# Attention with sixteen channels: the vector engine's pieces start two channels ahead, are computed with integer bit operations, and take 512 more columns

## The chip, the core and the metric

The kernel runs on one core of a Trainium2 chip. The metric is the device time of one execution in microseconds. The core has TensorE (PE, matrix products), VectorE (DVE), ScalarE (ACT, activation functions), GpSimd (POOL) and SyncE (SP, which issues DMAs). They run side by side and wait for each other through semaphores.

## The reference

What matters is the attention layer; a small feed-forward layer with experts follows it.

```python
cos_pm = jnp.cos(phase_modulators)              # 16 channels x 16 heads
def wl_step(acc, wl):
    cpm, iw = wl
    m = cpm[None, :, None, None]
    scores = jnp.einsum('bhqd,bhkd->bhqk', Q * m, K * m) * SCALE
    scores = scores * jnp.cos(KERR * scores * scores)
    attn = jax.nn.softmax(scores, axis=-1)
    out = jnp.einsum('bhqk,bhkd->bhqd', attn, V)
    return (acc + out * iw, None)
acc, _ = jax.lax.scan(wl_step, acc0, (cos_pm, interference_weights))
```

There are 8 batches, 16 heads, 512 positions and 8 dimensions per head. The cosine of the scores is one in single precision for these inputs, and the kernel has a branch for that case, which is the one that runs. So each channel w is exp(scores * c2[w, head]), normalised and multiplied by V: 16 exponentials of the same scores with different scales.

## The kernel before

**Units.** The work is cut into 32 units of one head and four batches: units 0 to 15 for the first four batches, 16 to 31 for the second four. A unit's scores lie in `s_t` as 8192 columns on 128 partitions (4 tiles of 128 keys, times 4 batches, times 512 queries), in one of two buffers. A unit has 15 steps, w = 0 to 14, one for each channel that ScalarE does.

**ScalarE.** At step w it computes the exponential of channel w into one of two buffers of `probs`: all 8192 columns for w = 0 to 13 (line 694). For w = 14 it computes fewer (line 691), `ACT_LAST`: 6144 in units 0 to 15, 6656 in units 16 to 31. Before it writes, it waits until TensorE has used the buffer's previous content, that of channel w - 2 (`pv_done`); before a unit it waits for the unit's scores (`st_copied`).

**VectorE's pieces.** Channel 15, and what ScalarE leaves of channel 14, are computed on VectorE by `piece_dve` in pieces of up to 2048 columns: four for channel 15 and a fifth for channel 14 (2048 or 1536 columns). A piece is seven operations, numbered 0 to 6 (lines 764, 767, 771, 775, 779, 783, 787): split the scaled score in a whole number and a fraction (0 to 2), a polynomial of the fraction (3 to 5), times the power of two (6). The pieces of a unit are numbered through, 35 operations, and a table says which of them stand in which step:

```python
PIECE_STEPS = {0: (0, 3), 1: (3, 5), 2: (5, 6), 3: (6, 8), 4: (8, 10), 5: (10, 12), 6: (12, 15), 7: (15, 18), 8: (18, 19),
               9: (19, 21), 10: (21, 22), 11: (22, 24), 12: (24, 27), 13: (27, 31), 14: (31, 35)}
PRODUCT_STEPS = {6: 0, 8: 1, 11: 2, WA: 3, WA + 1: 4}
COPY_STEPS = {2: 0, 5: 1, 8: 2, 11: 3, WA: 4, WA + 1: 5}
TURN_STEPS = {4: 0, 7: 1, 10: 2, 13: 3, WA + 1: 4, WA + 2: 5}
```

A step of WA (15) or more is one of the next unit.

**TensorE.** At step w it does the pieces' products that are due (`piece_pe`, line 800), then waits for ScalarE's channel w and does its 16 matmuls of 512 columns (line 1392; the trace records each matmul twice, so they are x32 there). Then it transposes a finished group of three channels (`turn_products`, line 1362), which VectorE has copied out of PSUM before (`copy_products`, line 1524) and normalises after (`weigh`, lines 1534 to 1552), and last it does its part of the preparation of the next unit.

**Preparation of the next unit.** It goes back and forth between TensorE and VectorE: projections (lines 829 and 906) at step 1, four score tiles and their maxima (846, 911) at steps 2 to 5, transposes at step 6 (852, 859; 915, 918), and four tiles of final scores and their copies to `s_t` (886, 923) at steps 8 to 11.

**Feed-forward in units 16 to 31.** The layer behind the attention is done for the first batches in between, at fixed steps (`FF_STEPS`). VectorE waits there for a short chain on GpSimd (lines 532 to 544) before line 1006.

Each engine runs its instructions strictly in the order in which the program writes them: in a step of VectorE, pieces, copies, `weigh`, preparation.

Of the kernel before, what the change touches and what calls it, by code (L numbers as in the profile page):

```python
# [15 lines left out]
P = 128  # L16
# [26 lines left out]
SHARED_B = (0, 1)  # L43
ACT_LAST = [T * X_COLS - (NB - b) * S for b in SHARED_B]
PIECES = T + 1
# [63 lines left out]
def postln_kernel(nc, a):  # L109
    with ExitStack() as ctx:  # L110
# [23 lines left out]
        x_2k = sb("x_2k", [P, X_COLS], BF16)  # L134
        x_n = x_2k[:].bitcast(I16)
# [82 lines left out]
        gate_b = scratch(G + EXPERTS)  # L218
        assert taken[0] <= T * NB * S
# [8 lines left out]
        one_row = sb("one_row", [P, P])  # L228
# [279 lines left out]
        def _(pool):  # L508
# [3 lines left out]
            nc.gpsimd.memset(one_row[:], 1.0)  # L512
# [241 lines left out]
        def piece_dve(dve, n, op, u, p, h):  # L754

            piece, base = u * PIECES + n, (u * PIECES + n) * PIECE_LINKS

            w, start, cols = (W - 1, n * X_COLS, X_COLS) if n < T else (WA - 1, ACT_LAST[u // H], T * X_COLS - ACT_LAST[u // H])
            scores = s_t[:, p, start:start + cols]
            scale = c2_last[:, w - (WA - 1), h:h + 1]  # L760
            at, y, t = x_n[:, 0:cols], x_y[:, 0:cols], x_p[:, piece % 2, 0:cols]
# [23 lines left out]
            if op == 6:  # L785
                dve.wait_ge(s["piece_chain"], base + 5)
                nc.vector.scalar_tensor_tensor(out=t, in0=t, scalar=EXP2_D, in1=x_2k[:, 0:cols], op0=ALU.add, op1=ALU.mult) \  # L787
                    .then_inc(s["piece_ready"], 1)

        def piece_pe(pe, n, u):  # L790

            pe.wait_ge(s["piece_ready"], u * PIECES + (n + 2))
# [553 lines left out]
        def _(pe):  # L1346
# [8 lines left out]
            with pe.If(fast == 1):  # L1355
# [10 lines left out]
                for u in range(UNITS):  # L1366
# [12 lines left out]

                    for w in range(WA):  # L1380
# [8 lines left out]
                        for kt in range(T):  # L1389
                            for b in range(SHARED_B[g] if w == WA - 1 and kt == T - 1 else NB):  # L1390
# [5 lines left out]
                                    stop=(w in LAST_OF and kt == (T - 2 if u == UNITS - 1 and w == WA - 1 and b >= SHARED_B[g] else T - 1)))  # L1396
# [24 lines left out]
        def _(dve):  # L1421
# [91 lines left out]
            with dve.If(fast == 1):  # L1513
                def copy_products(v, at):

                    wg = GROUP_AT[at]
                    if wg == NWG - 1:
                        dve.wait_ge(s["piece_used"], v * PIECES + (T + 1))
                    else:

                        dve.wait_ge(s["pv_done"], v * WA + (sum(W_GROUPS[wg]) + 3))
                        if wg == LAST_OF[WA - 1]:
                            dve.wait_ge(s["piece_used"], v * PIECES + (PIECES + 1))
# [35 lines left out]
                for u in range(UNITS):  # L1559
# [68 lines left out]
```

## Time and profile before

| | |
|---|---|
| three runs | 3397.57, 3400.41, 3402.31 us, median 3400.41 |
| the profiled execution | 3401.9 us, its span 3400.1 us |
| busy | ACT 98%, DVE 95%, PE 78%, POOL 7% |
| ScalarE, line 694 | 447 activations of 8192 columns |
| TensorE's mean granted clock | 0.942 of full speed |

The span is the time from the first to the last instruction of the profile. The loop over the units lies between about 38 us and 3320 us; some 80 us of feed-forward layer follow.

### The profile page before, as it was taken

How to read it: one execution, taken by the hardware profiler on the slowest of the kernel's cores; microseconds unless marked ns; L12 is line 12 of the kernel's file. 1: busy time of each engine (PE TensorE's matmuls, PEld its weight loads, DVE VectorE, ACT ScalarE, POOL GpSimd, SP SyncE). 2: the span in 40 equal slices, each digit the busy share in tenths (PEclk: the TensorE clock that was granted, in tenths of full speed). 3: DMA queues.
4: the chain of work that ended last, by engine and by line, in shares of the span. 5: the costliest groups of instructions: out<-in, count | busy, mean ns of one | idle time of the engine just before them, and what ended most of it. 6: DMA issues, size and time to landing. Idle time of an engine off the chain costs nothing.

```text
span 3400.1 us, 47604 instructions
## 1 busy us (share of the span) xinstructions
PE 2635.9 (78%) x20641; PEld 755.2 (22%) x20641; DVE 3235.6 (95%) x2740; ACT 3316.0 (98%) x612; POOL 230.5 (7%) x321
## 2 busy tenths in 40 slices
PE   7777877777777777777777778788888777777776
PEld 2212222212221222221222222222222222222224
DVE  7999999999999999999999999999999999999997
ACT  7999999999999999999999999999999999999992
POOL 0000000000000000000001111101111101111000
PEclk8999899999999989999999999988999999999988
DMA  1000000000000000000000000000000000000001
GB/s 50 1 1 1 1 1 1 1 1 1 1 1 1 1 1 1 1 15 1 1 1 3 4 2 4 2 1 4 2 4 3 4 1 2 4 2 16 1 18 31
DMA packets 21400, 16.05 MB, mean 5 GB/s; under 512 B 4865, under 2 KB 19602, under 8 KB 20946
## 3 DMA queue, kind: packets, MB, share of 16 engines
q1 hardware_dynamic: 19922, 12.28, 1.2%
q8 instruction: 165, 2.70, 0.3%
q10 hardware_dynamic: 1152, 0.53, 0.1%
q0 software_dynamic: 128, 0.26, 0.0%
q14 instruction: 33, 0.27, 0.0%
HBM read 7.70 MB, written 5.37 MB: 4 GB/s over the span
## 4 chain that ended last, share of the span: by engine, by line
ACT 59%; issue 33%; ACTq 4%; DVE 2%; PE 2%; DMA 0%; POOL 0%; DVEq 0%
ACT probs L694 55%; ACTq L684 4%; ACT probs L691 3%; PE psum L1392 0%; ACTq L688 0%; DVE s_t L923 0%; DMA probs<-in_L_attn_bv_dram 0%; DVE m_pad L911 0%; DVE probs L976 0%; DVE probs L1006 0%; PE psum L950 0%; PE psum L945 0%; PE psum L1093 0%; PE psum L935 0%; PE psum L1112 0%
## 5 line engine op out<-in xcount | busy, mean ns | idle before, releaser
L694 ACT ACTIVATE probs<-s_t 128x8192 f32<-128x8192 f32 x447 | 3100.4, 7070 | 2.5 <-PE psum L1392 2.5
L1392 PE MATMUL psum<-probs,v_pad 128*27 128x512 f32 x15136 | 1889.3, 640 | 644.2 <-ACT probs L694 609.2
L1392 PEld LDWEIGHTS psum<-probs,v_pad 128*27 128x27 f32 x15136 | 458.4, 112 | 1990.1 <-issue 1007.6
L767 DVE SCALAR_TENSOR_TENSOR x_y<-s_t,c_last,x_2k 128x2048 f32<-128x2048 f32 (+1 forms) x160 | 369.5, 2310 | 2.4
L779 DVE SCALAR_TENSOR_TENSOR x_p<-x_p,x_y 128x2048 f32<-128x2048 f32 (+1 forms) x160 | 358.2, 2239 | 4.5
L787 DVE SCALAR_TENSOR_TENSOR x_p<-x_p,x_2k 128x2048 f32<-128x2048 f32 (+1 forms) x160 | 357.7, 2236 | 3.9
L783 DVE SCALAR_TENSOR_TENSOR x_p<-x_p 128x2048 f32<-128x2048 f32 (+1 forms) x160 | 357.2, 2232 | 2.4
L775 DVE SCALAR_TENSOR_TENSOR x_p<-x_y 128x2048 f32<-128x2048 f32 (+1 forms) x160 | 356.4, 2227 | 0.0
L923 DVE COPY s_t<-psum 128x2048 f32<-128x2048 f32 x128 | 292.1, 2283 | 8.7 <-PE psum L886 8.4
L911 DVE TENSOR_REDUCE m_pad<-psum 128x4 f32<-128x2048 f32 x128 | 292.4, 2286 | 5.9 <-PE psum L846 4.7
L764 DVE TENSOR_SCALAR x_2k<-s_t,c_last 128x2048 int16<-128x2048 f32 (+1 forms) x160 | 201.1, 1257 | 4.9 <-issue 1.0
L800 PE MATMUL psum<-x_p,v_pad 128*27 128x512 f32 x1248 | 181.4, 600 | 7.7 <-DVE x_p L787 7.4
L846 PE MATMUL psum<-qkv_t 8*128 8x512 f32 x1024 | 149.8, 656 | 46.4 <-DVE m_pad L911 37.8
L691 ACT ACTIVATE probs<-s_t,ln_one 128x6144 f32<-128x6144 f32 (+1 forms) x32 | 181.4, 5668 | 0.0
L886 PE MATMUL psum<-qkv_t 9*128 9x512 f32 x1024 | 148.2, 649 | 1.7 <-DVE s_t L923 1.6
L1524 DVE TENSOR_SCALAR o_sb<-psum,iw_col 128x512 f32<-128x512 f32 x192 | 142.7, 743 | 3.0 <-PE psum L1392 3.0
L521 POOL COPY w_head<-w_qkv 128x24 f32 (+1 forms) x31 | 32.4, 1046 | 1633.6 <-ACT probs L694 1621.7
L1362 PE MATMUL psum<-ident,o_sb 128*128 128x128 f32 x768 | 126.0, 287 | 9.6 <-DVE o_sb L1524 8.1
L532 POOL TENSOR_TENSOR loop_memory<-loop_memory 128x2 f32<-128x2 f32 x24 | 35.0, 1458 | 1380.3 <-DVE loop_memory L976 1380.3
L1534 DVE RECIPROCAL r_z<-psum 128x48 f32<-128x48 f32 (+1 forms) x192 | 79.9, 416 | 50.6 <-PE psum L1362 50.5
L1362 PEld LDWEIGHTS psum<-ident,o_sb 128*128 128x128 f32 x768 | 80.6, 141 | 174.8 <-issue 138.5
L771 DVE TENSOR_SCALAR x_2k<-x_2k 128x2048 int16<-128x2048 int16 (+1 forms) x160 | 111.9, 699 | 5.5
(251 smaller groups left out, 1080.8 us busy)
## 6 DMA issues: line engine op xcount, KB each, us to landing
s_t<-in_L_attn_x_dram SPq DMA_DIRECT2D x4, 256.0 KB, 7.2
x_next_dram<-x_p SPq DMA_DIRECT2D x1, 1024.0 KB, 4.5
x_group<-x_next_dram SPq DMA_DIRECT2D x1, 1024.0 KB, 4.8
loop_memory<-in_L_attn_x_dram SPq DMA_DIRECT2D x8, 128.0 KB, 2.1
x_dram<-loop_memory SPq DMA_DIRECT2D x8, 128.0 KB, 1.8
out_dram<-loop_memory SPq DMA_DIRECT2D x8, 128.0 KB, 1.8
x_dram<-probs SPq DMA_DIRECT2D x2, 512.0 KB, 4.8
out_dram<-probs SPq DMA_DIRECT2D x2, 512.0 KB, 4.0
```

The lines of the kernel that those rows point to most:

```text
L691: nc.scalar.activation(probs[:, (p + w) % 2, 0:ACT_LAST[g]], s_t[:, p, 0:ACT_LAST[g]], ACT.Exp, bias=ln_one[:, 0:1], scale=scales[(p + w) ...
L694: nc.scalar.activation(probs[:, (p + w) % 2, :], s_t[:, p, :], ACT.Exp, scale=scales[(p + w) % 2]).then_inc(s["exp_done"], 1)
L764: nc.vector.tensor_scalar(at, scores, scale, LOWEST_Y, ALU.mult, ALU.max).then_inc(s["piece_chain"], 1)
L767: nc.vector.scalar_tensor_tensor(out=y, in0=scores, scalar=scale, in1=at, op0=ALU.mult, op1=ALU.subtract) \
L775: nc.vector.scalar_tensor_tensor(out=t, in0=y, scalar=EXP2_A, in1=y, op0=ALU.add, op1=ALU.mult) \
L779: nc.vector.scalar_tensor_tensor(out=t, in0=t, scalar=EXP2_B, in1=y, op0=ALU.add, op1=ALU.mult) \
L783: nc.vector.scalar_tensor_tensor(out=t, in0=t, scalar=EXP2_C, in1=t, op0=ALU.add, op1=ALU.mult) \
L787: nc.vector.scalar_tensor_tensor(out=t, in0=t, scalar=EXP2_D, in1=x_2k[:, 0:cols], op0=ALU.add, op1=ALU.mult) \
L911: nc.vector.tensor_reduce(m_pad[:, qt, :].rearrange("p (b l) -> p b l", l=L)[:, :, R_M:R_M + 1], banks(qt), AX.X, ALU.max, negate=True).th ...
L923: nc.vector.tensor_copy(s_t[:, p, kt * NB * S:(kt + 1) * NB * S], banks(kt).rearrange("p b q -> p (b q)")).then_inc(s["st_copied"], 1)
L1362: last = nc.tensor.transpose(psum[:, 6, qt * P:(qt + 1) * P], o_sb[:, at % 2, qt * P:(qt + 1) * P], ident[:])
L1392: last = nc.tensor.matmul(products_of(u, wg)[L * b:L * b + SLOTS * A, :], v_pad[:, p, b * T + kt, c0:c0 + SLOTS * A], probs[:, (p + w) % 2 ...
```

## The change

It changes four things.

1. **How a piece is split.** Operation 0 now writes the scaled score times 2^23 as a 32-bit integer (`x_i`, 2048 columns of int32, in place of `x_2k` with 16 bits). Operation 1, a SCALAR_TENSOR_TENSOR with two tensors, becomes a TENSOR_SCALAR that keeps the fraction bits and sets the exponent of one. Operation 2, a TENSOR_SCALAR on 16-bit data, becomes one on 32-bit data (`bitwise_xor`, `bitwise_and`). Operations 3 to 6 are as before with other constants; the last reads `x_i` as float.
2. **Who computes what of channel 14.** ScalarE computes 512 columns fewer in every unit: 5632 in units 0 to 15, 6144 in units 16 to 31. The fifth piece is 2048 columns in all units; units 0 to 15 have a sixth piece of 512 columns, whose product (one matmul) stands at step 0 of the next unit.
3. **When the pieces stand.** The tables now begin at step -2, two steps before the unit, and end at step 12. In unit 0, which has no unit before it, the operations of steps -2, -1 and 0 all stand in step 0. VectorE's first piece operation waits for `st_copied` of its unit, which VectorE itself has signalled.
4. A constant row for the experts moves from GpSimd's start to VectorE's part of the last unit.

```diff
-SHARED_B = (0, 1)
-ACT_LAST = [T * X_COLS - (NB - b) * S for b in SHARED_B]
-PIECES = T + 1
+SHARED_B = (3, 4)
+ACT_LAST = [(T - 1) * X_COLS - (NB - b) * S for b in SHARED_B]
...
-PIECE_STEPS = {0: (0, 3), 1: (3, 5), 2: (5, 6), 3: (6, 8), 4: (8, 10), 5: (10, 12), 6: (12, 15), 7: (15, 18), 8: (18, 19),
...
+SIX_STEPS = {-2: (0, 4), -1: (4, 7), 0: (7, 11), 1: (11, 12), 2: (12, 13), 3: (13, 16), 4: (16, 18), 5: (18, 20), 6: (20, 23),
...
+AHEAD = 2
+
+
+def pieces_due(u, w):
+
+    found = []
+    for v in (u, u + 1):
+        steps = steps_of(v, PIECE_STEPS, LAST_PIECE_STEPS) if v < UNITS else {}
+        at = w - (v - u) * WA
+        for step in range(-AHEAD if (u, v, w) == (0, 0, 0) else at, at + 1):
+            found += [(v, i) for i in range(*steps.get(step, (0, 0)))]
+    return found
...
             if op == 0:
+                if n == 0:
+                    dve.wait_ge(s["st_copied"], (u + 1) * T)
                 dve.wait_ge(s["piece_ready"], piece + 1)
                 nc.vector.tensor_scalar(at, scores, scale, LOWEST_Y, ALU.mult, ALU.max).then_inc(s["piece_chain"], 1)
             if op == 1:
                 dve.wait_ge(s["piece_chain"], base + 1)
-                nc.vector.scalar_tensor_tensor(out=y, in0=scores, scalar=scale, in1=at, op0=ALU.mult, op1=ALU.subtract) \
+                nc.vector.tensor_scalar(y.bitcast(I32), at, FRACTION_BITS, ONE_BITS, ALU.bitwise_and, ALU.bitwise_or) \
                     .then_inc(s["piece_chain"], 1)
             if op == 2:
                 dve.wait_ge(s["piece_chain"], base + 2)
-                nc.vector.tensor_scalar(at, at, 127.0, 128.0, ALU.add, ALU.mult)
+                nc.vector.tensor_scalar(at, at, EXPONENT_TOP, EXPONENT_BITS, ALU.bitwise_xor, ALU.bitwise_and)
...
-            for b in range(NB) if n < T else range(SHARED_B[u // H], NB):
-                at = b * S if n < T else (b - SHARED_B[u // H]) * S
+            first, latest = SHARED_B[u // H] if n > T else 0, pieces_of(u) - 1
+            for b in range(first, NB):
+                at = (b - first) * S
```

On VectorE, the start of unit 0 (the scores of unit 0 are there; line 906, now 941, is the preparation of unit 1 at step 1). Before:

```order
L764 TENSOR_SCALAR x_2k<-s_t,c_last 128x2048
L767 SCALAR_TENSOR_TENSOR x_y<-s_t,c_last,x_2k 128x2048
L771 TENSOR_SCALAR x_2k<-x_2k 128x2048
L775 SCALAR_TENSOR_TENSOR x_p<-x_y 128x2048
L779 SCALAR_TENSOR_TENSOR x_p<-x_p,x_y 128x2048
L906 TENSOR_TENSOR qkv_t<-psum,b_head 128x1536
```

And now:

```order
L801 TENSOR_SCALAR x_y<-x_i 128x2048
L805 TENSOR_SCALAR x_i<-x_i 128x2048
L809 SCALAR_TENSOR_TENSOR x_p<-x_y 128x2048
L813 SCALAR_TENSOR_TENSOR x_p<-x_p,x_y 128x2048
L817 SCALAR_TENSOR_TENSOR x_p<-x_p 128x2048
L821 SCALAR_TENSOR_TENSOR x_p<-x_p,x_i 128x2048
L798 TENSOR_SCALAR x_i<-s_t,c_last 128x2048
L801 TENSOR_SCALAR x_y<-x_i 128x2048
L805 TENSOR_SCALAR x_i<-x_i 128x2048
L809 SCALAR_TENSOR_TENSOR x_p<-x_y 128x2048
L813 SCALAR_TENSOR_TENSOR x_p<-x_p,x_y 128x2048
L941 TENSOR_TENSOR qkv_t<-psum,b_head 128x1536
```

One L798 stands ahead of these rows, so twelve piece operations stand before the line that frees TensorE's score tiles, where there were five.

On VectorE, the end of a unit among units 0 to 15, steps 11 and 12 (L958 is the last copy of the next unit's scores, before it was L923). Before:

```order
L923 COPY s_t<-psum 128x2048
L775 SCALAR_TENSOR_TENSOR x_p<-x_y 128x2048
L779 SCALAR_TENSOR_TENSOR x_p<-x_p,x_y 128x2048
L783 SCALAR_TENSOR_TENSOR x_p<-x_p 128x2048
L787 SCALAR_TENSOR_TENSOR x_p<-x_p,x_2k 128x2048
L764 TENSOR_SCALAR x_2k<-s_t,c_last 128x2048
```

And now:

```order
L958 COPY s_t<-psum 128x2048
L821 SCALAR_TENSOR_TENSOR x_p<-x_p,x_i 128x2048
L798 TENSOR_SCALAR x_i<-s_t,c_last 128x512
L801 TENSOR_SCALAR x_y<-x_i 128x512
L805 TENSOR_SCALAR x_i<-x_i 128x512
L809 SCALAR_TENSOR_TENSOR x_p<-x_y 128x512
L813 SCALAR_TENSOR_TENSOR x_p<-x_p,x_y 128x512
L817 SCALAR_TENSOR_TENSOR x_p<-x_p 128x512
L821 SCALAR_TENSOR_TENSOR x_p<-x_p,x_i 128x512
L798 TENSOR_SCALAR x_i<-s_t,c_last 128x2048
```

The sixth piece is done in one run, and the last row is the first operation of the next unit, at step 13.

On TensorE, steps 14 and 0 of a unit among units 0 to 15, the rows from the last group's transposes on. Before:

```order
L1362 MATMUL psum<-ident,o_sb 128x128 x4
L1392 MATMUL psum<-probs,v_pad 27x512 x12
L800 MATMUL psum<-x_p,v_pad 27x512 x4
L1392 MATMUL psum<-probs,v_pad 27x512 x16
L800 MATMUL psum<-x_p,v_pad 27x512 x4
```

And now:

```order
L1398 MATMUL psum<-ident,o_sb 128x128 x4
L835 MATMUL psum<-x_p,v_pad 27x512 x4
L1432 MATMUL psum<-probs,v_pad 27x512 x11
L835 MATMUL psum<-x_p,v_pad 27x512
L1432 MATMUL psum<-probs,v_pad 27x512 x32
```

Channel 14 has one matmul less of ScalarE's part, the fifth product moves ahead of it, and at step 0 only one matmul of a piece stands before channel 0's sixteen.

## Rows read from the trace of the kernel before

**Rows 1.** The page: busy us, share, instructions; TensorE's granted clock in 40 slices.
```profile
PE 2635.9 (78%) x20641; PEld 755.2 (22%) x20641; DVE 3235.6 (95%) x2740; ACT 3316.0 (98%) x612; POOL 230.5 (7%) x321
...
PEclk8999899999999989999999999988999999999988
```

**Rows 2.** Waits on ScalarE: who, for whom; us in total, times, longest.
```profile
ACT probs L694 <- PE psum L1392: 2.5, 2, 1.3
```

**Rows 3.** Timeline of ScalarE at two units' ends: start us, us, instruction.
```profile
1568.73 5.42 ACT L691 ACTIVATE probs<-s_t,ln_one 128x6144 f32<-128x6144 f32 x1
1574.04 7.04 ACT L694 ACTIVATE probs<-s_t 128x8192 f32<-128x8192 f32 x1
...
1875.99 5.87 ACT L691 ACTIVATE probs<-s_t,ln_one 128x6656 f32<-128x6656 f32 x1
1881.72 7.06 ACT L694 ACTIVATE probs<-s_t 128x8192 f32<-128x8192 f32 x1
```

**Rows 4.** Waits on VectorE, 147 to 1670 us, then 1670 to 3212 us.
```profile
DVE r_z L1534 <- PE psum L1362: 32.0, 19, 4.6
...
DVE loop_memory L1006 <- POOL loop_memory L544: 24.3, 14, 1.8
DVE r_z L1534 <- PE psum L1362: 12.6, 7, 3.1
```

**Rows 5.** Timeline of VectorE at step 10 of unit 14; in brackets idle before, releaser.
```profile
1552.39 0.46 DVE L1534 RECIPROCAL r_z<-psum 128x48 f32<-128x48 f32 x1 [2.38 <-PE psum L1362]
```

**Rows 6.** VectorE's groups by line and form: count, busy us, mean ns, idle before.
```profile
L767 DVE SCALAR_TENSOR_TENSOR x_y<-s_t,c_last,x_2k 128x2048 f32<-128x2048 f32 x144 | 340.4, 2364 | 1.8
...
L783 DVE SCALAR_TENSOR_TENSOR x_p<-x_p 128x2048 f32<-128x2048 f32 x144 | 329.1, 2285 | 1.9
...
L764 DVE TENSOR_SCALAR x_2k<-s_t,c_last 128x2048 int16<-128x2048 f32 x144 | 184.8, 1283 | 4.4 <-issue 1.0
...
L771 DVE TENSOR_SCALAR x_2k<-x_2k 128x2048 int16<-128x2048 int16 x144 | 102.9, 715 | 4.9
...
L783 DVE SCALAR_TENSOR_TENSOR x_p<-x_p 128x1536 f32<-128x1536 f32 x16 | 28.1, 1758 | 0.6
...
L1002 DVE SCALAR_TENSOR_TENSOR probs<-probs 128x16 f32<-128x16 f32 x9 | 1.6, 175 | 0.3
...
L996 DVE TENSOR_SCALAR probs<-probs 128x16 int32<-128x16 int32 x3 | 0.5, 175 | 0.1
...
L1002 DVE SCALAR_TENSOR_TENSOR probs<-probs 128x2 f32<-128x2 f32 x3 | 0.5, 161 | 0.1
...
L1443 DVE TENSOR_SCALAR probs<-probs 128x256 f32<-128x256 f32 x1 | 0.3, 294 | 0.0
...
L996 DVE TENSOR_SCALAR probs<-probs 128x2 int32<-128x2 int32 x1 | 0.2, 169 | 0.0
```

**Rows 7.** Timeline of VectorE and TensorE in unit 0.
```profile
44.41 1.29 DVE L764 TENSOR_SCALAR x_2k<-s_t,c_last 128x2048 int16<-128x2048 f32 x1 [0.97 <-issue]
45.73 2.35 DVE L767 SCALAR_TENSOR_TENSOR x_y<-s_t,c_last,x_2k 128x2048 f32<-128x2048 f32 x1
...
58.30 1.76 DVE L906 TENSOR_TENSOR qkv_t<-psum,b_head 128x1536 f32<-128x1536 f32 x1 [4.96 <-PE psum L829]
...
65.87 6.59 PE L1392 MATMUL psum<-probs,v_pad 128*27 128x512 f32 x32 [2.22 <-ACT probs L694]
```

**Rows 8.** Timeline at steps 0 and 2 of unit 1: the copy, channel 2's matmuls.
```profile
157.01 0.75 DVE L1524 TENSOR_SCALAR o_sb<-psum,iw_col 128x512 f32<-128x512 f32 x1
...
161.18 3.63 PE L1392 MATMUL psum<-probs,v_pad 128*27 128x512 f32 x32
```

**Rows 9.** Timeline of TensorE and ScalarE at the end of unit 3.
```profile
441.76 6.38 PE L1392 MATMUL psum<-probs,v_pad 128*27 128x512 f32 x32 [3.29 <-ACT probs L694]
...
448.22 27.81 ACT L694 ACTIVATE probs<-s_t 128x8192 f32<-128x8192 f32 x4 [1.21 <-PE psum L1392]
```

**Rows 10.** Timeline of GpSimd at step 14 of unit 18: the chain's first operation.
```profile
1987.43 1.63 POOL L532 TENSOR_TENSOR loop_memory<-loop_memory 128x2 f32<-128x2 f32 x1 [88.38 <-DVE loop_memory L976]
```

More of the change, by code:

```diff
@@ L42, with pieces_of, piece_no @@
 X_COLS = NB * S
-SHARED_B = (0, 1)
-ACT_LAST = [T * X_COLS - (NB - b) * S for b in SHARED_B]
-PIECES = T + 1
-LOG2_E = float(np.log2(np.e))
-LOWEST_Y = -126.0
-EXP2_A, EXP2_B, EXP2_C, EXP2_D = 5.5933580, 42.364143, 197.45122, 12068.066
-EXP2_ONE = 12068.069
+SHARED_B = (3, 4)
+ACT_LAST = [(T - 1) * X_COLS - (NB - b) * S for b in SHARED_B]
+def pieces_of(u):
+    return T + 1 + (SHARED_B[u // H] < NB)
+def piece_no(u, n):
+    return sum(pieces_of(v) for v in range(u)) + n
+LOG2_E = float(np.log2(np.e))
@@ new lines @@
+SIX_STEPS = {-2: (0, 4), -1: (4, 7), 0: (7, 11), 1: (11, 12), 2: (12, 13), 3: (13, 16), 4: (16, 18), 5: (18, 20), 6: (20, 23),
+             7: (23, 26), 8: (26, 27), 9: (27, 31), 10: (31, 32), 11: (32, 34), 12: (34, 42)}
+PIECE_STEPS = tuple(SIX_STEPS if b < NB else FIVE_STEPS for b in SHARED_B)
+FIVE_PRODUCTS = {3: 0, 6: 1, 9: 2, 12: 3, WA: 4}
+SIX_PRODUCTS = {3: 0, 6: 1, 9: 2, 12: 3, 14: 4, WA: 5}
+PRODUCT_STEPS = tuple(SIX_PRODUCTS if b < NB else FIVE_PRODUCTS for b in SHARED_B)
+COPY_STEPS = ({2: 0, 5: 1, 8: 2, 11: 3, WA: 4, WA + 1: 5},) * NG
@@ L73, in steps_of @@
 def steps_of(u, usual, last):
-    return last if u == UNITS - 1 else usual
+    return last if u == UNITS - 1 else usual[u // H]
 def due(u, w, usual, last):
@@ L754, in piece_dve @@
         def piece_dve(dve, n, op, u, p, h):
[L756 to L758 removed]
+            piece, base = piece_no(u, n), piece_no(u, n) * PIECE_LINKS
+            w, start, cols = ((W - 1, n * X_COLS, X_COLS) if n < T else (WA - 1, (T - 1) * X_COLS, X_COLS) if n == T
+                              else (WA - 1, ACT_LAST[u // H], (T - 1) * X_COLS - ACT_LAST[u // H]))
             scores = s_t[:, p, start:start + cols]
             scale = c2_last[:, w - (WA - 1), h:h + 1]
[L761 removed]
+            at, y, t = x_i[:, 0:cols], x_y[:, 0:cols], x_p[:, piece % 2, 0:cols]
             if op == 0:
+                if n == 0:
+                    dve.wait_ge(s["st_copied"], (u + 1) * T)
                 dve.wait_ge(s["piece_ready"], piece + 1)
@@ L1140, in experts_memory_dve @@
             nc.vector.memset(zx, 0.0)
+            nc.vector.memset(one_row, 1.0)
         def experts_weights_dve(dve):
@@ L1389, in _ @@
                         for kt in range(T):
-                            for b in range(SHARED_B[g] if w == WA - 1 and kt == T - 1 else NB):
+                            for b in range(NB if w < WA - 1 or kt < T - 2 else SHARED_B[g] if kt == T - 2 else 0):
                                 at = (kt * NB + b) * S
@@ L1395, in _ @@
                                     start=(kt == 0 and w in FIRST_OF),
-                                    stop=(w in LAST_OF and kt == (T - 2 if u == UNITS - 1 and w == WA - 1 and b >= SHARED_B[g] else T - 1)))
+                                    stop=(w in LAST_OF and kt == T - 1) or (w == WA - 1 and kt == T - 2 and products_end_here(u)))
                         last.then_inc(s["pv_done"], 1)
@@ L1564, in _ @@
                     for w in range(WA):
-                        if w in steps_of(u, PIECE_STEPS, LAST_PIECE_STEPS):
-                            for i in range(*steps_of(u, PIECE_STEPS, LAST_PIECE_STEPS)[w]):
-                                piece_dve(dve, i // PIECE_OPS, i % PIECE_OPS, u, p, u - g * H)
+                        for v, i in pieces_due(u, w):
+                            piece_dve(dve, i // PIECE_OPS, i % PIECE_OPS, v, v % 2, v % H)
                         for v, at in due(u, w, COPY_STEPS, LAST_COPY_STEPS):
```

43 lines of the change are left out of this document (24 added, 19 removed).

## The prediction

> **What bounds the kernel now.** I read the page first: ScalarE is busy 98% of the span, VectorE 95%, and TensorE 78% [rows 1]. Shares alone don't say who sets the pace, so next come the waits. ScalarE, in 32 units of exponentials, waits for TensorE twice, 2.5 us in all [rows 2]; within the loop it never waits for anything else. So the loop lasts as long as ScalarE's activations, and a column taken from it comes off the time, as long as the two others keep up. TensorE waits for ScalarE in nearly every step and has room. VectorE is the open question. In units 1 to 15 its waits are 32 us, nearly all at one place, the third `weigh` at step 10 [rows 4]: it arrives there 2.38 us early [rows 5]. That is all the room that it has in a unit. In units 16 to 31 it waits for TensorE 12.6 us, 1.6 for each of the eight pairs of units, and 24.3 us in 14 waits, 1.74 each, for GpSimd's chain [rows 4]; the chain's latency is no room.
>
> **What the change takes from ScalarE.** The timeline gives the period of the last activation, start to start: 1574.04 - 1568.73 = 5.31 us with 6144 columns, 1881.72 - 1875.99 = 5.73 us with 6656 [rows 3]. 512 columns are 0.42 us. All 32 units lose 512: 32 x 0.42 = **-13.4 us**. Full activations follow each other every (27.81 - 7.06) / 3 = 6.92 us [rows 3, 9], so a unit goes from 14 x 6.92 + 5.31 = 102.2 to 101.8 us.
>
> **What it does to VectorE's load.** A piece of 2048 columns now costs 1.283 + 2.364 + 0.715 + 4 x 2.285 = 13.50 us [rows 6]. New are operations 1 and 2, bitwise TENSOR_SCALARs on int32; no row has one of this size. Two TENSOR_SCALARs, L764 and L771, show that one source goes faster than two, which takes (2285 - 1758) / 512 = 1.03 ns a column: L764 is 1.0 us below L783 at equal columns. Does a bit operation on int32 do so too? The small rows answer: L996 is a logical shift of int32 and grows by 6 ns from 2 to 16 columns, 0.43 ns a column, while the two-source L1002 grows by 14 ns, 1.0 a column [rows 6]. So I take half of 1.03, from L1443 (294 ns at 256 columns, constants in the instruction as here): 0.294 + 1792 x 0.515 ns = 1.22 us. The ends are this and the full rate, 1.22 + 2048 x 0.515 ns = 2.27 us, as if it had two sources; I take the low one because of L996.
>
> The Trainium skill, "VectorE: DVE Perf Modes", section "What auto-detection actually checks", says that the engine picks its two-port mode from the number of sources and where they lie, and that firmware caps what an op may use; it says nothing of bitwise ops. By its table a four-byte TENSOR_SCALAR of 2048 columns would be 1.23 us, and no run here shows the bitwise form yet.
>
> With 1.22 a piece is 1.283 + 2 x 1.22 + 9.14 = 12.86 us, 0.64 less.
> - Units 0 to 15: five pieces save 3.2. The sixth has 512 columns: by the same slopes 0.49 + 2 x 0.43 + 4 x 0.70 = 4.15, and seven gaps of 0.03 to 0.04 between dependent operations (44.41 + 1.29 to 45.73, [rows 7]) make 4.4. Net +1.2 us. The room goes from 2.38 to 2.38 - 1.2 - 0.42 = **0.76 us a unit**.
> - Units 16 to 31: four pieces save 2.56. The fifth was 13.50 less 512 columns of five two-source operations, one at half and one at a quarter of the rate (3.0), so 10.5; it becomes 12.86. Net -0.2 a unit. The room of a pair goes from 1.6 to 1.6 + 0.3 - 0.84 = 1.1 us.
> So VectorE still keeps up, and its cost in the sum is **0**. The cover is thin: at 1.30 us for the bitwise operations instead of 1.22 it is gone in the first half.
>
> **GpSimd's chain.** At step 14 VectorE runs three operations of 2.29 us in place of four of 1.76, and then waits for the chain. The chain's first operation lasted 1.63 us, and three after it the same [rows 10], each about one operation of VectorE. The Trainium skill, "SBUF — State Buffer", section "SBUF: two separate sides", explains it: GpSimd and a two-source VectorE operation share a port, and one holds it for its whole instruction. By that rule the chain's blocked steps get longer with 2048 columns, three of 2.3 in place of four of 1.7, and VectorE's wait stays near 1.9 us; if the port didn't matter, it would stay at 1.74. Either is inside the room of 1.1 a pair (twice 0.2 more). Sum: 0.
>
> **Unit 0.** Twelve piece operations now stand ahead of line 906: from 44.41, one piece (12.86 and gaps, 13.1) and five more (1.28 + 2.44 + 4.57 and gaps, 8.4) end at 65.9, and line 906 ends at 67.6, not at 60.1 [rows 7]. TensorE's next score tile, the first piece's product (which moves to step 3) and channel 3's matmuls stand behind it. ScalarE wants the buffer for channel 5 at 65.87 - 0.15 + 6.92 = 72.6. It waits 0.8 to 3.7 us. TensorE idles before this product again, so I take **+3.5**. ScalarE can't recover it. Later units have 15 steps for this and don't show it.
>
> **TensorE's slow moments.** Both waits of ScalarE are at a unit's end: channel 13's matmuls took 6.38 us instead of 3.63 after 3.29 us of idling [rows 9]; channel 14's activation is short, so channel 0 of the next unit waited 1.21. That activation is now 0.42 shorter: **+0.8** for the two. Elsewhere the margins stay close: at step 0 VectorE's copy comes at about its old place (in steps 11 to 0 stand 14 large operations and the small piece, before 16 large ones; -3.7 and +4.4), channel 2's matmuls end at 164.8 [rows 8] and ScalarE needs them at 65.7 + 14 x 6.92 + 5.31 = 167.9. I allow **+0.3** for a slow moment that now shows. TensorE's work stays the same.
>
> **The end.** The last unit has 12 matmuls behind the last activation instead of 13: **-0.2**. The row of ones on VectorE is one small memset in the last unit, where VectorE waits anyway: 0.
>
> **Sum.** -13.4 + 3.5 + 0.8 + 0.3 - 0.2 = -9.0 us. Against the profiled execution's 3401.9 us that is 3392.9. The median of the runs is 1.5 lower, so I predict **3391.4 us**. Its own range: unit 0 from 0.8 to 3.7 and slow moments from -2.5 (both waits vanish) to +7 (one such wait every fourth unit or so) give -15 to -3: 3386 to 3398.
>
> **Rivals.**
> - *VectorE becomes the bound.* If the bitwise operations run at the full rate, 2.27 us, each piece costs 2.1 more, a unit 10.5. After the room of 0.76 it is 9.8 us in each of 16 units and 20 in each of 8 pairs, 316 us, less 13.4: about 3700 us. For it: no row shows the operation at size. Against it: L996's slope. It decides from 1.30 us an operation on. 7%.
> - *VectorE's order makes TensorE late in every unit.* The place is the copy at step 0, on which the transposes, the projections and channel 2's matmuls queue. There is 167.9 - 164.8 = 3.1 us of room; were the copy 4 us later in each unit, ScalarE would lose 0.9 x 32 = 29 us: 3400.4 - 13.4 + 29 = 3416. The count above says that it comes within 1 us of its place. 6%.
> - *The gain is given back in small waits.* With 0.76 us of room VectorE reaches its transposes and score maxima later than before, TensorE waits for it in more steps, and each slow moment of up to 3 us then reaches ScalarE. One of 1.5 us in every fifth unit is 10 us: 3396 to 3400. For it: the granted clock is lower in seven of the 40 slices than in the rest (8 tenths for 9) [rows 1], and two slow moments already reach ScalarE [rows 2]. 15%.
> - *The whole gain arrives.* Unit 0 costs 0.8 and no new wait appears: 3387.6. 8%.
> - The forecast: 64%.
>
> **Chances.** A measurement of this kernel can tell about 0.2%, 6.8 us, from no change. The forecast (but for 2% at its upper end) and the whole gain are faster, 70%; the small waits, that 2% and 1% of the second rival are the same, 18%; the rest is slower, 12%. The range takes in the small waits and stops before the slow cases: 3385.5 to 3401.
>
> **What would show it.** Lines 801 and 805 near 1.22 us (wrong: above 1.3). ScalarE's last period 4.89 us in units 0 to 15 and 5.31 after. ScalarE's first wait at channel 5 of unit 0, up to 3.7 us, and few others, at channel 0 and after slow matmuls. VectorE's wait at step 10 shrunk from 2.38 to about 0.8. If VectorE shows no wait at all in the first half and ScalarE waits once in each unit, VectorE is the bound and the forecast is wrong.

## The result and the profile after

The changed kernel takes 3406.85 us (median of 20 runs, 3403.03 to 3409.69), the kernel before 3400.37 us (20 runs beside it). The ratio is 1.0018 [1.0012, 1.0024]: 6.5 us slower, where 9.0 us faster was forecast. The profiled execution took 3406.8 us, its span is 3405.0 us.

The page of the changed kernel, busy us and the granted clock. In 15 of the first 20 slices the clock is 8 tenths, where [rows 1] has three such slices:

```profile
PE 2693.3 (79%) x20641; PEld 776.3 (23%) x20641; DVE 3247.3 (95%) x2853; ACT 3305.6 (97%) x612; POOL 239.4 (7%) x320
...
PEclk8889888889888889889999999999999999999987
```

Two stretches of the changed kernel, units 1 to 15 and units 16 to 31 (windows: width, busy us of PE, PEld, DVE, ACT, POOL, then TensorE's granted clock):

```profile
100.00:1683.00 1583.00, 1289.75 (x9760) 350.44 (x9760) 1537.32 (x1208) 1576.23 (x233) 8.85 (x30) 0.90 0.01 2
1683.00:3320.00 1637.00, 1271.98 (x10129) 362.39 (x10133) 1560.47 (x1298) 1630.32 (x248) 220.66 (x261) 0.95 0.01 4
```

The same windows of before have 0.95 and 0.94. The work on TensorE is the same (9752 matmul records in the first stretch before, 9760 now), yet it is busy 1289.8 us there and not 1212.5.

ScalarE's waits within the loop, to be read against [rows 2], and TensorE's for one copy of VectorE, which was 8.1 us in 10 waits before:

```profile
ACT probs L725 <- PE psum L1432: 15.4, 23, 2.8
...
PE psum L1398 <- DVE o_sb L1564: 55.3, 29, 3.5
```

**The account of the time.** These rows of ScalarE are the first full activation of the loop and the last short one, in the changed kernel and then in the kernel before:

```profile
43.68 7.02 ACT L725 ACTIVATE probs<-s_t 128x8192 f32<-128x8192 f32 x1
...
3317.20 5.40 ACT L722 ACTIVATE probs<-s_t,ln_one 128x6144 f32<-128x6144 f32 x1
```

```profile
44.95 7.02 ACT L694 ACTIVATE probs<-s_t 128x8192 f32<-128x8192 f32 x1
...
3314.45 5.93 ACT L691 ACTIVATE probs<-s_t,ln_one 128x6656 f32<-128x6656 f32 x1
```

The loop starts 1.3 us earlier (no effect of the change that these runs could show: in the runs below it starts anywhere between 42.1 and 44.3 us). Between the two rows lie 3273.5 us and not 3269.5, though 31 short activations are 0.42 us shorter each (13.0): ScalarE loses 4.0 + 13.0 = 17.0 us more than before. From start to start of each activation these 17 us lie, against before: 2.9 at channel 5 of unit 0; 7.7 at the unit ends (10.4, before 2.7); 5.8 ahead of channel 4 in units 16 to 31, nearly all in units 18, 20, 24 and 26; 0.6 elsewhere. After the last short activation stand 3405.0 - 3317.20 = 87.8 us and not 85.65; as this activation is itself 0.5 shorter, the end costs 2.7. Sum: -1.3 + 4.0 + 2.2 = +4.9 us, the difference of the spans. (The medians differ by 6.5, since the profiled execution of the kernel before lies 1.5 above its median.)

**The unit ends.** At the end of a unit ScalarE does channel 14, which is short, and then needs for channel 0 of the next unit the buffer that channel 13 filled; TensorE must be done with it by then. The end of unit 4 of the changed kernel, ScalarE's timeline, and TensorE's: channel 13's 16 matmuls, 32 records.

```profile
545.73 4.99 ACT L722 ACTIVATE probs<-s_t,ln_one 128x5632 f32<-128x5632 f32 x1
551.19 97.05 ACT L725 ACTIVATE probs<-s_t 128x8192 f32<-128x8192 f32 x14 [0.47 <-PE psum L1432]
```

```profile
545.89 5.22 PE L1432 MATMUL psum<-probs,v_pad 128*27 128x512 f32 x32 [3.03 <-ACT probs L725]
```

ScalarE needs the buffer that these matmuls read after 4.89 us (the period at the end of unit 14, the one where they took 3.64: 1569.70 to 1574.59), and they hold it for 5.22. The period is 551.19 - 545.73 = 5.46, so 0.57 us is lost. The granted clock of TensorE in 545.9 to 551.1 was 0.69: part of the group ran at the lower level of 1.2 GHz. Of the 16 unit ends of units 0 to 15, 15 have a slow group like this one. Its length grows from 4.97 us in unit 0 through 5.10, 5.17 and 5.21 to 5.22 in unit 4 and stays there (5.22 or 5.23) up to unit 13. From start to start these 15 lose 0.32 to 0.67 us each, 8.1 of the 10.4. Before, two of the 16 were slow (one in [rows 9]); most were like this one of unit 8, fast after a wait of the same length:

```profile
954.20 3.64 PE L1392 MATMUL psum<-probs,v_pad 128*27 128x512 f32 x32 [3.29 <-ACT probs L694]
```

In units 16 to 30 of the changed kernel nine more ends are slow (5.33 us). There channel 14's activation covers them nearly: they lose 0.25 us each, the other 2.2 us. Over both stretches, groups of channels 0 to 13 that lasted over 3.9 us in place of 3.64 have become 136, before 88, in the first stretch 90, before 35. They now come back at the same channels of each unit, and units last 102.4 us from one to the next (545.73, 648.13, ...), where 14 x 6.92 + 4.89 = 101.8 was to be had.

**The copies.** The start of unit 18, VectorE and then TensorE and ScalarE:

```profile
1895.82 2.28 DVE L821 SCALAR_TENSOR_TENSOR x_p<-x_p,x_i 128x2048 f32<-128x2048 f32 x1
1898.14 1.30 DVE L798 TENSOR_SCALAR x_i<-s_t,c_last 128x2048 int32<-128x2048 f32 x1
1899.48 1.63 DVE L801 TENSOR_SCALAR x_y<-x_i 128x2048 int32<-128x2048 int32 x1
1901.15 1.23 DVE L805 TENSOR_SCALAR x_i<-x_i 128x2048 int32<-128x2048 int32 x1
1902.29 0.74 DVE L1564 TENSOR_SCALAR o_sb<-psum,iw_col 128x512 f32<-128x512 f32 x1
```

```profile
1903.09 0.66 PE L1398 MATMUL psum<-ident,o_sb 128*128 128x128 f32 x4 [3.46 <-DVE o_sb L1564]
1903.68 4.48 PE L864 MATMUL psum<-x_group,w_head 128*32 128x512 f32 x24
1907.97 3.62 PE L1432 MATMUL psum<-probs,v_pad 128*27 128x512 f32 x32
```

```profile
1911.66 7.04 ACT L725 ACTIVATE probs<-s_t 128x8192 f32<-128x8192 f32 x1 [1.88 <-PE psum L1432]
```

The copy of channel 15's product now stands behind four large operations after the wait for GpSimd (L1041); before it stood behind three. TensorE waits 3.46 us for it (before 0.92 here), then the projections take 4.48 and not 2.78, and channel 2's matmuls end at 1911.6, 1.88 too late. The late copy alone isn't enough: at the start of unit 22 TensorE waits for it nearly as long, but the projections are fast, and ScalarE doesn't wait.

```profile
2315.49 0.66 PE L1398 MATMUL psum<-ident,o_sb 128*128 128x128 f32 x4 [3.01 <-DVE o_sb L1564]
2316.08 2.78 PE L864 MATMUL psum<-x_group,w_head 128*32 128x512 f32 x24
```

In all seven even units from 18 to 30 TensorE waits 2.6 to 3.5 us for the copy, and ScalarE waits in the four (18, 20, 24, 26) in which the projections took 4.08 to 4.48 us. Each of these waits goes with both, a late copy and a slow moment behind it.

**The end.** One row of TensorE in the tail, the experts' matmuls, 3.60 before:

```profile
3363.40 6.16 PE L1147 MATMUL psum<-s_t,probs 128*128 128x512 f32 x8
```

It explains 2.56 of the 2.7 us.

### The profile page after: what moved, and what is told of

It is laid out like the page before. It is cut to its first block, busy times and chain, and to the rows that moved or that the text cites. A ratio compares the mean times of both kernels' runs of the same rounds, so it can differ in the third digit from the quotient of the medians.

```text
span 3405.0 us, 47748 instructions
## 1 busy us (share of the span) xinstructions
PE 2693.3 (79%) x20641; PEld 776.3 (23%) x20641; DVE 3247.3 (95%) x2853; ACT 3305.6 (97%) x612; POOL 239.4 (7%) x320
## 4 chain that ended last, share of the span: by engine, by line
issue 45%; ACT 40%; PE 5%; POOL 4%; DVE 3%; ACTq 3%; DMA 0%; POOLq 0%; DVEq 0%
ACT probs L725 39%; PE psum L1432 4%; ACTq L715 2%; POOL loop_memory L565 1%; POOL loop_memory L563 1%; POOL loop_memory L567 1%; POOL loop_memory L575 0%; ACTq L719 0%; ACT probs L722 0%; POOL loop_memory L614 0%; DVE s_t L958 0%; PE psum L864 0%; DVE x_p L813 0%; DVE m_pad L946 0%; DVE probs L1011 0%
## 5 line engine op out<-in xcount | busy, mean ns | idle before, releaser
L725 ACT ACTIVATE probs<-s_t 128x8192 f32<-128x8192 f32 x447 | 3099.6, 7024 | 16.3 <-PE psum L1432 15.4
L1432 PE MATMUL psum<-probs,v_pad 128*27 128x512 f32 x15072 | 1948.3, 662 | 583.6 <-ACT probs L725 574.7
L809 DVE SCALAR_TENSOR_TENSOR x_p<-x_y 128x2048 f32<-128x2048 f32 x176 | 376.1, 2137 | 19.4 <-PE psum L835 19.2
L817 DVE SCALAR_TENSOR_TENSOR x_p<-x_p 128x2048 f32<-128x2048 f32 x176 | 377.3, 2144 | 4.1
L821 DVE SCALAR_TENSOR_TENSOR x_p<-x_p,x_i 128x2048 f32<-128x2048 f32 x176 | 377.3, 2144 | 3.3
L813 DVE SCALAR_TENSOR_TENSOR x_p<-x_p,x_y 128x2048 f32<-128x2048 f32 x176 | 376.8, 2141 | 2.4
L958 DVE COPY s_t<-psum 128x2048 f32<-128x2048 f32 x128 | 291.7, 2280 | 4.2 <-PE psum L921 4.2
L798 DVE TENSOR_SCALAR x_i<-s_t,c_last 128x2048 int32<-128x2048 f32 x176 | 215.6, 1225 | 6.2 <-issue 1.0
L801 DVE TENSOR_SCALAR x_y<-x_i 128x2048 int32<-128x2048 int32 x176 | 206.3, 1172 | 6.1
L805 DVE TENSOR_SCALAR x_i<-x_i 128x2048 int32<-128x2048 int32 x176 | 202.4, 1150 | 3.9
L722 ACT ACTIVATE probs<-s_t,ln_one 128x5632 f32<-128x5632 f32 (+1 forms) x32 | 166.2, 5195 | 0.0
L881 PE MATMUL psum<-qkv_t 8*128 8x512 f32 x1024 | 148.7, 651 | 21.2 <-DVE m_pad L946 15.5
L864 PE MATMUL psum<-x_group,w_head 128*32 128x512 f32 x768 | 96.9, 635 | 0.0
```

Of the source, the lines that this page charges most:

```text
L725: nc.scalar.activation(probs[:, (p + w) % 2, :], s_t[:, p, :], ACT.Exp, scale=scales[(p + w) % 2]).then_inc(s["exp_done"], 1)
L801: nc.vector.tensor_scalar(y.bitcast(I32), at, FRACTION_BITS, ONE_BITS, ALU.bitwise_and, ALU.bitwise_or) \
L805: nc.vector.tensor_scalar(at, at, EXPONENT_TOP, EXPONENT_BITS, ALU.bitwise_xor, ALU.bitwise_and)
L809: nc.vector.scalar_tensor_tensor(out=t, in0=y, scalar=EXP2_A, in1=y, op0=ALU.add, op1=ALU.mult) \
L813: nc.vector.scalar_tensor_tensor(out=t, in0=t, scalar=EXP2_B, in1=y, op0=ALU.add, op1=ALU.mult) \
L817: nc.vector.scalar_tensor_tensor(out=t, in0=t, scalar=EXP2_C, in1=t, op0=ALU.add, op1=ALU.mult) \
```

## The experiments

Theory 1: TensorE's slow moments have settled on channel 13, where the shortened activation of channel 14 no longer covers them. Theory 2: VectorE's order puts the copies late. Rivals: the bitwise operations, or too little room on VectorE. All ratios are to the kernel before on the same chip.

| run | median us | ratio, 95% interval | ScalarE's waits for TensorE in the loop, us (times) |
|---|---|---|---|
| changed kernel | 3406.85 | 1.0018 [1.0012, 1.0024] | 15.4 (23) |
| bits | 3401.29 | 1.0001 [0.9992, 1.001] | 1.2 (1) |
| copy14 | 3399.58 | 0.9999 [0.999, 1.0008] | 12.4 (16) |
| fill13 | 3405.98 | 1.0012 [1.0003, 1.0021] | 18.2 (16) |
| s44 | 3404.4 | 1.0013 [1.0004, 1.0022] | 6.2 (7) |
| c_fill | 3391.27 | 0.9976 [0.9966, 0.9986] | 4.3 (2) |
| c_first | 3399.6 | 0.9998 [0.9989, 1.0007] | 9.3 (18) |
| all | 3390.12 | 0.997 [0.9958, 0.9983] | 3.2 (4) |
| c_fill0 | 3400.35 | 1.0 [0.9991, 1.0009] | 12.2 (15) |
| c_s44 | 3398.75 | 0.9994 [0.9985, 1.0003] | 1.7 (4) |
| bits_fill | 3398.74 | 0.9993 [0.9984, 1.0002] | none |

**bits**: the kernel before with operations 0, 1, 2 and 6 of a piece as in the change, and nothing else of it.

> The kernel before with the new operations of a piece alone (bitwise operations on 32-bit integers, their constants, one_row in scratch), its old tables and its old split of channel 14. Theory 1 (TensorE's slow moments have settled on channel 13 at the end of the units, where channel 14's activation of 4.88 us is now shorter than the slow group of 5.22): no change from before, 3400 (3398 to 3402), since channel 14's activation stays at 5.31. Theory 2 (VectorE's order puts the copies of steps 0 and 1 behind more of a piece): also 3400. Rival, the cost comes with the bitwise operations: 3404 to 3407.

No change. The bitwise operations cost nothing, and the 0.64 us a piece that they save is worth nothing where VectorE has room.

**copy14**: the changed kernel, one number of one table.

```diff
-COPY_STEPS = ({2: 0, 5: 1, 8: 2, 11: 3, WA: 4, WA + 1: 5},) * NG
+COPY_STEPS = ({2: 0, 5: 1, 8: 2, 11: 3, 14: 4, WA + 1: 5},) * NG
```

> The changed kernel with the copy of channel 15's product moved from step 0 of the next unit to step 14, so that TensorE's transposes at step 0 no longer stand behind three or four operations of a piece. Theory 2: the 55 us in which TensorE waits for that copy go, with them the ScalarE waits ahead of channel 4 in units 18, 20, 24 and 26 (5.8 us), about 3401, and lower (3393 to 3399) if that idle time is also what makes TensorE slow at channel 13. Theory 1 alone: the waits at the ends of units 0 to 15 (0.5 to 0.6 us each) stay, 3401 to 3407. Rival, VectorE has too little room: no gain, 3407.

7.3 us come back by the medians, 6.1 between the two profiled executions: 5.8 ahead of channel 4 and 1.7 in the tail, less 1.4 more in unit 0. No wait for this copy and none ahead of channel 4 is left in the trace. The unit ends stay as they were: 14 waits of 0.57 to 0.58 and one of 0.15; unit 0's wait is 4.20. One unit end of this run, ScalarE and TensorE:

```profile
1366.83 4.97 ACT L722 ACTIVATE probs<-s_t,ln_one 128x5632 f32<-128x5632 f32 x1
1372.38 7.04 ACT L725 ACTIVATE probs<-s_t 128x8192 f32<-128x8192 f32 x1 [0.57 <-PE psum L1432]
```

```profile
1366.98 5.33 PE L1432 MATMUL psum<-probs,v_pad 128*27 128x512 f32 x32 [3.28 <-ACT probs L725]
```

So theory 2 holds for 5.8 us of the loss, and the slow channel 13 doesn't come from the late copy. Here it takes 5.33 us, the period is 1372.38 - 1366.83 = 5.55, and 0.66 us is lost against 4.89.

**fill13**: the changed kernel with work for TensorE where it idled.

```diff
+                        if w == 13 and u + 1 < UNITS:
+                            pe.wait_ge(s["st_copied"], (u + 2) * T)
+                            for _ in range(2):
+                                nc.tensor.matmul(prep[:, 0, 0:11 * (A + 2 * VPAD)], ident[:],
+                                                 v_pad[:, p, 0:11, :].rearrange("p j e -> p (j e)"), start=True, stop=True)
                         pe.wait_ge(s["exp_done"], u * WA + (w + 1))
```

> The changed kernel with two matmuls of 495 columns (some 0.9 us each, result never read) ahead of TensorE's wait for channel 13, where it stands idle for 3.03 us in every unit. Theory 1: the 16 matmuls of channel 13 take 3.64 us in place of 5.22, ScalarE's 15 waits at the unit ends (7.7 us of lost time over before) go, about 3399; if the slow moments settle at another channel it costs nothing there, since each other activation takes 6.92. Theory 2 alone: no change, 3407, or later. Rival, TensorE's matmuls are slow for want of something other than its clock: 3407 with channel 13 still at 5.22.

The median missed by 7 us. The eleven executions are spread wider than any other run's, 3398.05 to 3410.2, so some do reach the 3399; the profiled one took 3407.87, and its trace says why. No ScalarE wait is left at a unit's end, as theory 1 had it. But the waits ahead of channel 4 have grown to 15 in number and 14.5 us, up to 3.19. Unit 10 of this run, TensorE, then ScalarE:

```profile
1064.72 5.33 PE L1437 MATMUL psum<-probs,v_pad 128*27 128x512 f32 x32 [4.01 <-ACT probs L725]
1071.64 3.63 PE L1437 MATMUL psum<-probs,v_pad 128*27 128x512 f32 x32 [1.59 <-ACT probs L725]
1078.23 0.66 PE L1398 MATMUL psum<-ident,o_sb 128*128 128x128 f32 x4 [2.96 <-DVE o_sb L1569]
1078.82 4.48 PE L864 MATMUL psum<-x_group,w_head 128*32 128x512 f32 x24
```

```profile
1086.80 7.04 ACT L725 ACTIVATE probs<-s_t 128x8192 f32<-128x8192 f32 x1 [1.36 <-PE psum L1437]
```

With channel 13 fast, the slow moments settle elsewhere in the unit. In unit 10 and the units 11 to 15 after it the projections behind the late copy take 4.48 us, which none of them does in the changed kernel (2.78), and all six have a wait ahead of channel 4. The expectation's sentence that a slow moment costs nothing at another channel was wrong there: behind a late copy there is no room for one. I had not forecast this: each of the two causes hides part of the other.

**s44**: the changed kernel without the sixth piece, `SHARED_B = (4, 4)`.

> The changed kernel without the sixth piece: 6144 columns of channel 14 on ScalarE in every unit, five pieces on VectorE. ScalarE has 512 columns more in 16 units, 16 x 0.43 = 6.9 us. Theory 1: channel 14's activation of 5.31 covers the slow group of 5.22, the unit-end waits (7.7) go, and the sum is nought, 3404 to 3407; so the 512 columns are worth nothing in the changed kernel. Theory 2: 3407 + 6.9 = 3413 less what the lighter VectorE gives. Rival, VectorE's load is what costs: 3399 to 3402.

3404.4, as theory 1 has it: with 6.9 us more work the kernel is no slower (2.5 us less by the medians, but the intervals of the two ratios overlap). No unit-end wait is above 0.15 us, and four ahead of channel 4 are of the same sizes as in the changed kernel (1.91, 0.97, 1.93, 0.98, now in units 18, 20, 26 and 28). Channel 13 is slow in 13 of the first 16 units. In the kernel of the run bits, which in this half differs from s44 only in the tables of steps for pieces and their products, it is slow in two.

**c_fill, c_first, all, c_fill0**: combinations on top of copy14. c_fill adds the matmuls of fill13. c_fill0 adds them at step 0, ahead of channel 0. c_first has a table of its own for unit 0, all has this table and the matmuls:

```diff
+FIRST_PIECE_STEPS = {0: (0, 3), 1: (3, 6), 2: (6, 8), 3: (8, 11), 4: (11, 14), 5: (14, 17), 6: (17, 21), 7: (21, 24), 8: (24, 27),
+                     9: (27, 30), 10: (30, 32), 11: (32, 34), 12: (34, 42)}
...
-        steps = steps_of(v, PIECE_STEPS, LAST_PIECE_STEPS) if v < UNITS else {}
+        steps = FIRST_PIECE_STEPS if v == 0 else steps_of(v, PIECE_STEPS, LAST_PIECE_STEPS) if v < UNITS else {}
```

> Both edits of the last two runs: the copy of channel 15's product at step 14, and two extra matmuls ahead of TensorE's wait for channel 13. In the run with the copy alone 15 waits of 0.57 us were left at the unit ends (8.6) and one of 4.20 in unit 0; in the run with the matmuls alone the unit-end waits were gone and 11 us of waits stood ahead of channel 4, behind late copies. Theory (two causes, TensorE's slow moment at channel 13 and the copies put late by VectorE's order, each of which hides behind the other's repair): 3399.6 - 8.6 = 3391 (3389 to 3394), with one wait left, in unit 0. Rival, TensorE's slow moments only move to the next place that can't bear them: 3397 to 3402, with waits at another channel.

> The copy at step 14, and in unit 0 a table of its own that spreads the first pieces over steps 0 to 8 in place of ten operations at step 0. Theory: the 4.20 us wait ahead of channel 4 in unit 0 goes, 3395.3 (3393 to 3397), the unit-end waits stay. Rival, TensorE's slow moments come elsewhere after another unit 0, since what went before decides where they fall: anything from 3391 to 3400 with another number of unit-end waits.

> All three edits: the copy at step 14, two extra matmuls ahead of channel 13, unit 0's operations spread. Theory: 3391 - 4.2 = 3387 (3384 to 3390), faster than both kernels; ScalarE has no wait above 0.2 us in the loop. Rival (slow moments move): 3393 to 3399.

> Control: the copy at step 14, and the two extra matmuls at step 0 of every unit, ahead of channel 0, in place of channel 13; the same added work at a place where a slow group costs nothing, since the next activation takes 6.92. Theory: channel 13 stays slow and the unit-end waits of 0.57 stay, 3399 to 3401. Rival, any added work on TensorE keeps its clock up: 3391.

c_fill came out where two independent causes put it, at 3391.3. A unit end of it, TensorE and ScalarE:

```profile
1355.17 1.93 PE L1426 MATMUL psum<-v_pad,ident 128*128 128x495 f32 x4
1358.34 3.64 PE L1437 MATMUL psum<-probs,v_pad 128*27 128x512 f32 x32 [1.24 <-ACT probs L725]
```

```profile
1358.20 4.98 ACT L722 ACTIVATE probs<-s_t,ln_one 128x5632 f32<-128x5632 f32 x1
1363.08 13.93 ACT L725 ACTIVATE probs<-s_t 128x8192 f32<-128x8192 f32 x2
```

The period is 4.88, and the granted clock within the group 1.00. Two waits are left, 2.88 in unit 0 and 1.43 ahead of channel 4 of unit 19. The control c_fill0, on the same chip, has the same matmuls at another place: 14 unit-end waits of 0.57 stay, and no time is won; c_fill is 9.1 us faster than it. So it is the place and not the amount of work. c_first missed: the wait of 4.20 in unit 0 (it stands at channel 5; the expectation names the wrong channel) went, but 0.26, 0.93 and 0.81 came at channels 12 and 14 and in unit 1, with matmul groups of up to 6.58 us, and a gain of 4.3 was expected where none shows in the medians. `all` missed too: 3390.12 (six executions, 3385.01 to 3394.13), just outside its 3384 to 3390, and in place of no wait above 0.2 us it has 0.25 and 0.93 in unit 0, 0.65 ahead of unit 1 and 1.44 in unit 19. So spreading unit 0's operations brought no gain that shows, with the matmuls or without.

**c_s44, bits_fill**: copy14 without the sixth piece, and the kernel before with the bitwise operations and the matmuls at channel 13.

> The copy at step 14, and no sixth piece: 6144 columns of channel 14 on ScalarE in every unit. Against the run with the copy alone (3399.6) ScalarE has 16 x 0.43 = 6.9 us more work, and the 15 unit-end waits of 0.57 (8.6) should go, since 5.31 covers the slow group of channel 13. Theory: 3398 (3396 to 3400), so the 512 columns are worth less than nothing as long as channel 13 is slow, and 7 us with the two extra matmuls. Rival, the unit-end waits come from something that the sixth piece does to TensorE or VectorE and not from the shorter activation: also 3398, but channel 13's groups would then no longer be slow; the theory has them slow and covered.

> The kernel before with the bitwise operations and the two extra matmuls ahead of channel 13. Theory: channel 14's activation of 5.31 already covers a slow channel 13 and only two waits of 1.2 to 1.4 us were there to win, 3399 to 3401, no change. Rival, more work on TensorE is good by itself: 3392 to 3396.

c_s44 came out as expected; bits_fill is 0.3 us below its range, and no change from before either, as its theory has it. A unit end of c_s44, ScalarE and TensorE, slow and covered:

```profile
339.28 5.41 ACT L722 ACTIVATE probs<-s_t,ln_one 128x6144 f32<-128x6144 f32 x1
344.83 7.03 ACT L725 ACTIVATE probs<-s_t 128x8192 f32<-128x8192 f32 x1
```

```profile
339.43 5.33 PE L1432 MATMUL psum<-probs,v_pad 128*27 128x512 f32 x32 [3.29 <-ACT probs L725]
```

Channel 13 took 5.33 us in 10 of the first 16 units, and no wait above 0.15 us came of it. But the period of this slow end is 344.83 - 339.28 = 5.55 us, the same as in copy14 with 512 columns less. So 6144 columns don't cover the slow group quite: it costs 0.24 us against 5.31, and with 5632 columns 0.66 against 4.89. At such an end the 512 columns are worth nothing at all. This is the change's new order, without its sixth piece: the order makes channel 13 slow, and the split decides how much of it ScalarE sees. The old order with the new split, the fourth combination, was not run. In bits_fill no channel 13 is slow and ScalarE never waits for TensorE, and its median is 2.6 us below that of bits, whose trace has one wait of 1.2 us at a unit end.

## Why the prediction was wrong

- **What bounds the kernel, and what the change takes from ScalarE (-13.4): right.** At unit ends without a slow group the periods are 4.89 and, in the second half, 5.30. The loop's account closes with 0.42 a unit.
- **VectorE's load (0): right.** Rows of the changed kernel by form, count, busy us, mean ns:

```profile
L801 DVE TENSOR_SCALAR x_y<-x_i 128x2048 int32<-128x2048 int32 x160 | 199.5, 1247 | 5.5
L805 DVE TENSOR_SCALAR x_i<-x_i 128x2048 int32<-128x2048 int32 x160 | 195.6, 1223 | 3.4
...
L801 DVE TENSOR_SCALAR x_y<-x_i 128x512 int32<-128x512 int32 x16 | 6.8, 427 | 0.6
```

  1.22 and 0.43 us were predicted, from the slope of two small rows. The Trainium skill's table in "VectorE: DVE Perf Modes", section "Side-by-side: where the cycles go for N=2048 bf16", has 1224 ns for 2048 bf16 columns at two elements a cycle, and the trace agrees for 32-bit bitwise operations (1223 at L805). VectorE never became the bound. In units 1 to 15 it waits 22.8 us, 1.5 a unit where 0.76 was expected, and mostly at another place: 12 waits of 1.6 us ahead of L809, for TensorE to free a piece buffer.
- **GpSimd's chain (0): right in size.** VectorE waits 2.0 us for it (28.0 us, 14 times), 1.9 expected. In unit 18 the chain's long operations before step 0 are three of 2.17 to 2.25 us, where [rows 10] has one of 1.63 and three of 1.71 to 1.75 follow it, as the prediction had it.
- **Unit 0 (+3.5): right.** ScalarE waited 2.84 us at channel 5, inside 0.8 to 3.7. The slow moment came earlier than it was put: the score tile and the product took 2.09 and 1.93 us, counted at 0.9 each, and channel 3's matmuls 4.24, counted at 6.59.

```profile
74.33 7.04 ACT L725 ACTIVATE probs<-s_t 128x8192 f32<-128x8192 f32 x1 [2.84 <-PE psum L1432]
```

- **TensorE's slow moments at the unit ends (+0.8): the step that failed first.** It measured +7.7. I took the two slow groups of before as the number of slow groups after, and made each cost 0.42 more. The sentence "TensorE's work stays the same" is true of the work and not of when it idles: with the new order 15 of 16 unit ends are slow. And the 0.42 us took away a cover that I hadn't put a number to: 5.31 nearly hides a group of 5.22 or 5.33 (0.15 us of wait, 0.25 from start to start), and 4.89 does not. A slow group at the end of units 0 to 15 now costs 0.32 to 0.67 us, mostly 0.57. Rival 3 named it ("each slow moment then reaches ScalarE") but with one in five units, and laid it to VectorE's lateness at transposes and score maxima. copy14 shows that the late copy ahead of the transposes is not its cause, and for the maxima TensorE waits less than before (15.5 us at L881, 37.8 before).
- **"At step 0 VectorE's copy comes at about its old place" (+0.3 for what might show): failed.** It measured +5.8. I compared sums of operations over steps 11 to 0; what matters is what stands between the wait for GpSimd and the copy, four large operations now and three before. The room of 3.1 us was read where nothing was slow. In unit 18 TensorE waited 2.5 us longer for the copy, and its projections then took 1.7 longer, together 4.2. The lateness alone stays inside the 3.1 us of room; the slow projections behind it are what the room lacked. The place of rival 2 was right, its "in every unit" was not: four units pay.
- **The end (-0.2): +2.7**, or +1.4 with the start, 1.3 us earlier, which I didn't have either. The same eight matmuls took between 3.60 and 6.16 us in runs whose tail is the same, so this term probably is where the slow moment happens to fall. No run changed the tail, and its cause is only argued.

What is shown: the split by s44 against the changed kernel, the copy's place by copy14, and the order by s44 against bits, in the first half. What stays open is why the new order makes channel 13 slow: the idle time ahead of the group is 3.03 us now and was 3.29 before, when the group was fast. The Trainium skill, "TensorE: Matmul & The Clock Gate", section "HAM oscillation — how this bites in real kernels", tells of a kernel in which a wait in every tile makes each next tile start slow; the traces agree in that TensorE idles ahead of each slow channel 13 here, in a fixed rhythm, and that two matmuls in this gap end it. But a gap of this length doesn't make a slow group by itself: after idle times of 2.9 to 3.3 us 18 of 33 groups are slow in the kernel before and 44 of 58 in the changed one, and which it will be I can't work out from the rows.

## What to carry to other kernels

Before you shorten an instruction, ask what it covers: here the shortest activation of a unit lasted as long as a slow matmul group under it (5.31 against 5.22 to 5.33, at most 0.15 us of wait), and 0.42 us less turned a nearly harmless slow moment into a loss at each unit end that ate the gain there. Number such covers with the slow duration of the work beneath them and not with its usual one. When operations are moved ahead on a queue, look for the short ones on which another engine's chain hangs and put them first; one table entry was worth 7 us. And where an engine idles in a rhythm just ahead of work that is on the critical path, a little work whose result nobody reads can pay there (8.3 us for 62 matmuls), but run the control with the same work elsewhere. Remove such causes together as well as one by one: fill13 alone won nothing in its median, and on top of copy14 the same matmuls won 8.3 us.

## What the hardware did that I hadn't expected

- The slow groups lock to the program. In the changed kernel they stand at the same channels of each unit, 102.4 us apart, and copy14 keeps 102.5 between its waits (1064.9, 1167.4, 1269.9, 1372.4), while in the kernel before, with units of 102.2 us, they drift: channel 0 is slow in 13 of the first 15 unit starts after unit 0, with 5.13, 5.22, 5.30, then 3.64 and 6.52, and again 4.92, 5.00, 5.09 and on. In the changed kernel channel 13's group and with it the unit get longer for five units, and then the pattern stands still (4.97 to 5.22). That the waits themselves pull the unit to the length at which it stands still is read from these rows; no run tests it.
- 32-bit bitwise TENSOR_SCALARs are as fast as the float one at L798: 1223 and 1247 ns for 2048 columns, there 1299. The one at L801 took 1.63 us in place of 1.23 at the start of the seven even units from 18 to 30, each time with a GpSimd operation at the same time, as L771 took 1.11 for 0.69 in the kernel before.
- Two matmuls of 495 columns, 0.96 us each, ahead of a group: its granted clock was 1.00 in c_fill, 0.69 in the changed kernel and 0.68 in copy14 without them.
